# Two graph layers on one core: other places for ScalarE's copies, three last additions, the value products and the third pair's score tiles

## The chip, the cores and the metric

One core of one Trainium2 chip runs the whole kernel. The time is the device time of one execution in microseconds (us). Engines: TensorE (PE in the profile, its weight loads PEld), VectorE (DVE), ScalarE (ACT), GpSimd (POOL) and SyncE (SP, which issues the DMAs).

## The reference

There are 16 graphs of 512 nodes with 384 features, and two layers that are each added to their input. In outline:

```python
h = relu(layernorm(x));  x = x + attention(h, adj)
h = relu(layernorm(x));  x = x + graph_attention(h, adj)

# attention: 6 heads of 64 features
scores = q @ k.T / 8;  probs = softmax(where(adj, scores, -9e15))
out = (probs @ v) @ Wf + bf

# graph_attention: 12 heads of 32 features
hh = h @ W;  src = tanh(hh) . w_src;  dst = tanh(hh) . w_dst
attn = softmax(where(adj, leaky_relu(src_i + dst_j, 0.2), -999))
feat = elu(attn @ hh + b);  gate = sigmoid(h @ H_w.T + H_b)
out = gate * feat + (1 - gate) * h
```

## The kernel before, in words

The loop over graphs is software-pipelined. For graph b, `layer2(b)` runs the second layer, and in its spare places the first layer's query products, value products and first score tiles of graph b + 1. Then `attention(b + 1)` runs the first layer's attention, and in its spare places the end of graph b (the elu and the gate) and the key products of graph b + 2. There is one such round per graph. Each engine has its own program, written out by hand in the same function names, and waits on semaphores: an engine does its steps strictly in the written order.

The names that matter here, with the engine that does each step:

- The six heads of the attention are three **pairs** p = 0, 1, 2, and the 512 nodes four **tiles** t. `scores(g, p, t)` (PE, L1156) makes the two score tiles of a pair, called s(p,t) below; `maxima` (DVE, L822, two instructions) adds the mask and takes the row maximum; `exps` (ACT, L576, two instructions) takes the exponential and its sum; `inverse` (DVE, L828) inverts the sum; `normalise` (POOL, L416, two instructions) multiplies by it.
- `turn_probs(p, c)` (PE, L1173, 16 small transposes), called turn(p,c) below, turns column block c of the pair's probabilities into two PSUM banks, work0 and work1. DVE and ACT each empty one of them with a `pT_copy` (L832 and L582), and `context(p, c)` (PE, L1190, four matmuls), called ctx(p,c), multiplies by the values. The next turn needs both copies, since there is one pair of banks. `ctx_high` (ACT, L588) and `ctx_low` (DVE, L838) split a pair's result in two.
- `turn_norm` (PE, L1114), `turned_high` (ACT, L550) and `turned_low` (DVE, L799) turn the normalised input of the next graph; `query_key(p, "k")` (PE, L1099, nine matmuls) makes its keys, k0 to k2, which `qk_hi_copy` (ACT, L557) and `qk_low` (DVE, L807) split.
- The end of a graph, per tile: `positive` (DVE, L886), `elu` (ACT, L601), `difference` (DVE, L891), `add_out` (POOL, L458 and L460, the last addition) and a store.
- In `layer2`: `gate_product` (PE, L1099), `spread` (PE, L1233), 12 aggregation steps n, each with `edges` (DVE, L867, three instructions), `last_maxima` (ACT, L614 and L617), `last_edge` (POOL, L450) and `aggregate` (PE, L1252 and L1258, 16 matmuls); after the steps `sums_copy` (ACT, L625), `turn_sums(t)` (PE, L1271), `inverse_den` and `divide` (DVE, L873 and L878). `values(t)` (PE, L1099, nine matmuls of 384 columns) makes the next graph's values, and `value` (ACT, L562) empties them. `tanh_gate` is L605.

Eight PSUM banks hold everything. `HOME` (L41) says which of six shared banks a result goes to, and the lists `LAYER2` (L88) and `S_AFTER` (L62) in which order a bank's users follow each other; each user waits until the user before it has been drained. Values 3 and the sums of tile 1 share bank 0, values 2 and the sums of tiles 2 and 3 share bank 1.

In PE's program the scores of the next pair are spread over the turns by a table, and only the first turn of a pair waits for the probabilities, for all eight of them at once:

```python
S_AFTER = {(0, 0): ((1, 1), (1, 2)), (0, 1): ((1, 3),), (0, 3): ((2, 0), (2, 1)), (1, 0): ((2, 2),), (1, 1): ((2, 3),)}
...
                if c == 0:
                    pe.wait_ge(probs_ready, b * NS + tile_no(p, TT - 1, 1) + 1)
```

## Time and profile before

| | |
|---|---|
| median of 3 runs | 1788.58 us (1787.78 to 1788.93) |
| profiled execution, its own time | 1789.52 us |
| its span in the profile | 1787.7 us |
| busy: PE, DVE | 1669.8 us (93%), 1331.6 us (74%) |
| busy: ACT, POOL | 1102.6 us (62%), 1035.6 us (58%) |
| mean granted TensorE clock | 0.991 of full speed |

The profile is of one execution, and times in it count from the span's start. The busy time of an engine is the sum of its instructions; matmuls overlap, so PE's busy share is no measure of how much of its peak is used. What a step costs is read in the timeline: when it began, how long the engine had been idle before it, and for whom it had waited.

### The profile page before, as it was taken

How to read it: one execution, taken by the hardware profiler on the slowest of the kernel's cores; microseconds unless marked ns; L12 is line 12 of the kernel's file. 1: busy time of each engine (PE TensorE's matmuls, PEld its weight loads, DVE VectorE, ACT ScalarE, POOL GpSimd, SP SyncE). 2: the span in 40 equal slices, each digit the busy share in tenths (PEclk: the TensorE clock that was granted, in tenths of full speed). 3: DMA queues.
4: the chain of work that ended last, by engine and by line, in shares of the span. 5: the costliest groups of instructions: out<-in, count | busy, mean ns of one | idle time of the engine just before them, and what ended most of it. 6: DMA issues, size and time to landing. Idle time of an engine off the chain costs nothing.

```text
span 1787.7 us, 34621 instructions
## 1 busy us (share of the span) xinstructions
PE 1669.8 (93%) x12528; PEld 1021.7 (57%) x12528; DVE 1331.6 (74%) x3130; ACT 1102.6 (62%) x2231; POOL 1035.6 (58%) x1287
## 2 busy tenths in 40 slices
PE   6899999999999999999999999999999999999885
PEld 4474655647465574655657465574655746556462
DVE  4778687786878768677786877768777786876856
ACT  2666566675666656566665666666566665666653
POOL 4356565674656656565564646646575565655735
PEclk9899999999999999999999999999999999999997
DMA  4000101001010010100001010010100101000000
GB/s 156 19 19 11 50 7 37 19 16 45 7 54 7 15 40 8 54 7 25 30 12 50 7 37 25 11 44 7 54 7 15 41 12 50 7 19 19 10 10 18
DMA packets 38248, 48.24 MB, mean 27 GB/s; under 512 B 2624, under 2 KB 38080, under 8 KB 38080
## 3 DMA queue, kind: packets, MB, share of 16 engines
q1 hardware_dynamic: 38080, 46.03, 8.0%
q8 instruction: 102, 1.67, 0.4%
q14 instruction: 66, 0.54, 0.1%
HBM read 33.44 MB, written 12.58 MB: 26 GB/s over the span
## 4 chain that ended last, share of the span: by engine, by line
PE 74%; DVE 12%; ACT 6%; issue 3%; POOL 2%; DMA 0%; SPq 0%; DVEq 0%; POOLq 0%
PE work L1099 16%; PE score L1099 16%; PE acc L1258 8%; PE acc L1190 6%; PE acc L1252 6%; PE score L1156 6%; ACT arena L576 5%; PE work L1173 5%; DVE arena L867 4%; DVE sm L822 3%; PE work L1252 3%; POOL arena L416 2%; PE acc L1211 2%; PE score L1233 2%; PE score L1114 1%
## 5 line engine op out<-in xcount | busy, mean ns | idle before, releaser
L867 DVE SCALAR_TENSOR_TENSOR arena<-score,uqT,adjT 128x512 f32<-128x512 f32 x576 | 389.2, 745 | 33.3 <-PE score L1233 22.7
L416 POOL TENSOR_SCALAR arena<-arena,rinv 128x512 f32<-128x512 f32 x384 | 280.3, 746 | 186.1 <-DVE rinv L828 186.1
L576 ACT ACTIVATE arena<-sm,nmax 128x512 f32<-128x512 f32 x384 | 273.3, 714 | 126.2 <-DVE nmax L822 124.9
L450 POOL TENSOR_TENSOR arena<-arena,adjT 128x512 f32<-128x512 f32 x192 | 223.9, 1166 | 122.6 <-ACT arena L617 118.3
L822 DVE CUSTOM_DVE_ANT_0 sm<-score,mask 128x512 f32<-128x512 f32 x384 | 247.6, 685 | 56.8 <-issue 30.2
L1173 PEld LDWEIGHTS work<-ident_f,arena 64*128 64x128 f32 x3072 | 114.8, 140 | 180.8 <-issue 180.8
L1258 PE MATMUL acc<-arena,u_den 128*3 128x512 f32 x1536 | 200.8, 592 | 0.0
L1190 PE MATMUL acc<-arena,v_tok 128*64 128x512 f32 x768 | 197.7, 614 | 0.0
L423 POOL TENSOR_TENSOR rstd<-var,mhalf 128x1 f32<-128x1 f32 x128 | 68.7, 549 | 218.2 <-DVE var L786 218.2
L614 ACT ACTIVATE arena<-score,nqT 128x512 f32<-128x512 f32 x192 | 129.9, 677 | 100.8 <-PE score L1233 73.3
L1173 PE MATMUL work<-ident_f,arena 64*128 64x64 f32 x3072 | 138.0, 229 | 55.3 <-ACT arena L582 34.2
L832 DVE COPY arena<-work 128x512 f32<-128x512 f32 x192 | 130.9, 682 | 63.8 <-PE work L1173 63.7
L582 ACT ACTIVATE arena<-work 128x512 f32<-128x512 f32 x192 | 112.7, 587 | 94.0 <-PE work L1173 92.5
L1252 PE MATMUL acc<-arena 128*32 128x512 f32 x1024 | 135.2, 599 | 11.4 <-DVE arena L867 9.5
L617 ACT ACTIVATE arena<-arena,uqT 128x512 f32<-128x512 f32 x192 | 138.8, 723 | 6.2
L458 POOL TENSOR_TENSOR fin_g<-arena 128x384 f32<-128x384 f32 x64 | 69.1, 1080 | 114.1 <-DVE arena L891 113.7
L1258 PEld LDWEIGHTS acc<-arena,u_den 128*3 128x3 f32 x1536 | 42.4, 86 | 117.8 <-issue 117.8
L443 POOL TENSOR_TENSOR arena<-arena,uqT 128x384 f32<-128x384 f32 x64 | 61.3, 957 | 80.8 <-DVE uqT L1016 80.8
L1156 PE MATMUL score<-qk_hi 64*128 64x512 f32 x384 | 95.0, 481 | 5.2 <-DVE nmax L822 3.8
L544 ACT ACTIVATE hn<-xres,shift,rstd 128x384 f32<-128x384 f32 x64 | 45.4, 710 | 78.4 <-DVE shift L791 77.0
L807 DVE SCALAR_TENSOR_TENSOR qk_lo<-score,bias_c,qk_hi 128x512 fp32r<-128x512 f32 x64 | 47.9, 749 | 51.5 <-ACT qk_hi L557 51.5
L799 DVE SCALAR_TENSOR_TENSOR hT_lo<-score,hT_hi 128x384 fp32r<-128x384 f32 x112 | 59.0, 552 | 30.3 <-ACT hT_hi L550 30.2
(168 smaller groups left out, 3954.5 us busy)
## 6 DMA issues: line engine op xcount, KB each, us to landing
x_in<-in_x SPq DMA_DIRECT2D x16, 768.0 KB, 4.8
xb<-in_x SPq DMA_DIRECT2D x16, 768.0 KB, 4.6
out_x<-xres SPq DMA_DIRECT2D x64, 192.0 KB, 1.9
adj_u<-in_adj SPq DMA_DIRECT2D x16, 256.0 KB, 2.8
arena<-in_wk SPq DMA_DIRECT2D x1, 576.0 KB, 6.2
arena<-in_wq SPq DMA_DIRECT2D x1, 576.0 KB, 7.2
arena<-in_wv SPq DMA_DIRECT2D x1, 576.0 KB, 8.6
arena<-in_wf SPq DMA_DIRECT2D x1, 576.0 KB, 9.6
```

The lines of the kernel that those rows point to most:

```text
L416: nc.gpsimd.tensor_scalar(pr, pr, rinv[:, p, t, i:i + 1], 1.0, ALU.mult, ALU.mult).then_inc(probs_ready, 1)
L450: nc.gpsimd.tensor_tensor(edge_at(n, HG - 1), t_ring[:, n % 2], adjT[:, n % TT], ALU.mult).then_inc(last_edge_ready, 1)
L576: nc.scalar.activation(probs[p % 2 * 2 + i][:, t], sm[:, n % NSM], ACT.Exp, scale=-1.0, bias=nmax[:, p, t, i:i + 1], accum_out=rsum[:, p, ...
L617: nc.scalar.activation(t_ring[:, n % 2], t_ring[:, n % 2], ACT.Identity, bias=uqT[:, c, DROW + h:DROW + h + 1]).then_inc(max_ready, 1)
L822: mark_drained(nc.vector.tensor_tensor_reduce(sm[:, n % NSM], bank_of(g, "s", p, t, i)[:], mask[:, t], 1.0, 3.0e38, ALU.add, ALU.min, nmax ...
L867: nc.vector.scalar_tensor_tensor(out=edge_at(n, j), in0=score[j][:], scalar=uqT[:, c, q:q + 1], in1=adjT[:, c], op0=ALU.max, op1=ALU.mult) ...
L1099: ins = nc.tensor.matmul(ps, l(c), r(c), start=(c == 0 and i == 0), stop=(c == FC - 1 and i == 2))
L1156: ins = nc.tensor.matmul(bank_of(g, "s", p, t, i)[:], l[rows, 0, p, q], r[rows, 1, p], start=(n == 0), stop=(n == len(terms) - 1))
L1173: ins = nc.tensor.transpose(bank_of(b, "turn", p, c, half)[:, at:at + DH0], probs[p % 2 * 2 + i][rows, t, c * P:(c + 1) * P], ident_f[rows ...
L1190: ins = nc.tensor.matmul(acc[p % 2][i * DH0:(i + 1) * DH0], v_tok[:, c, f:f + DH0], pT[c % 2][:, i], start=(c == 0), stop=(c == TT - 1))
L1252: ins = nc.tensor.matmul(num[j * DH1:(j + 1) * DH1], h_tok[:, c, f:f + DH1], edge_at(n, j), start=(c == 0), stop=(c == TT - 1), skip_group ...
L1258: ins = nc.tensor.matmul(acc[1][j * DH1:j * DH1 + NG], u_den[:, c, g, j], edge_at(n, j), start=(n == 0), stop=(n == STEPS - 1), skip_group ...
```

## The change

Nothing is computed in another way; steps change places, and one wait is cut in pieces.

- **Value products.** `values(0)` goes from after aggregation step 5 to before step 0, `values(1)` from after the loop to after step 5. ScalarE's `value(0)` and `value(1)` follow, and its three later `tanh_gate` steps go to after steps 2, 3 and 6. Values 0 get bank 0.
- **After the loop.** PE makes s(0,3) before the sums of tile 1, and the sums of tiles 1 and 2 one after the other before values 3; VectorE does the maxima of s(0,3) before the division of tile 1.
- **Score tiles.** The third pair's tiles s(2,0) to s(2,3) come one after each of turn(0,3), turn(1,0), turn(1,1) and turn(1,2); two used to follow turn(0,3).
- **Copies.** ScalarE alternates exps and `pT_copy`.
- **Last additions.** `positive`, `elu`, `difference` and `add_out` of tiles 1 to 3 move towards the third pair.
- **The first turn of a pair** waits for each probability tile before that tile's transposes, and turns no longer raise a counter after their waits.

```diff
...
 
+TANH_AT = {2: 1, 3: 2, 6: 3}
+
 SPREADS = (3, 0, 1, 2)
...
     ("k", 0): 2, ("k", 1): 3, ("k", 2): 5, ("q", 0): 1, ("q", 1): 4, ("q", 2): 1,
-    ("v", 0): 1, ("v", 1): 1, ("v", 2): 1, ("v", 3): 0,
+    ("v", 0): 0, ("v", 1): 1, ("v", 2): 1, ("v", 3): 0,
     ("out", 0): 3, ("out", 1): 4, ("out", 2): 5, ("out", 3): 0,
...
 
-S_AFTER = {(0, 0): ((1, 1), (1, 2)), (0, 1): ((1, 3),), (0, 3): ((2, 0), (2, 1)), (1, 0): ((2, 2),), (1, 1): ((2, 3),)}
+S_AFTER = {(0, 0): ((1, 1), (1, 2)), (0, 1): ((1, 3),), (0, 3): ((2, 0),), (1, 0): ((2, 1),), (1, 1): ((2, 2),), (1, 2): ((2, 3),)}
 NORM_AFTER = {(0, 2): (0, 1), (1, 2): (2, 3)}
...
              ("feat", 0), ("feat", 1), ("feat", 2), ("tok", 0), ("tok", 1), ("tok", 2), ("tok", 3),
-             ("gate", 0), ("gate", 1), ("uq", 0), ("gate", 2), ("gate", 3), ("q", 2), ("num", 1), ("v", 0)]
-          + both("s", 0, 0) + both("s", 0, 1) + [("v", 1), ("fin", 0)] + both("s", 0, 2) + [("v", 2), ("fin", 1)]
-          + both("s", 0, 3) + [("fin", 2), ("v", 3), ("fin", 3)] + both("s", 1, 0))
+             ("gate", 0), ("gate", 1), ("uq", 0), ("gate", 2), ("gate", 3), ("v", 0), ("q", 2), ("num", 1), ("v", 1)]
+          + both("s", 0, 0) + both("s", 0, 1) + [("fin", 0)] + both("s", 0, 2) + [("v", 2)] + both("s", 0, 3)
+          + [("fin", 1), ("fin", 2), ("v", 3), ("fin", 3)] + both("s", 1, 0))
 START_UP = ([("norm1", t) for t in range(TT)]
...
                     add_out(g - 1, 0)
-                normalise(g, 2, 0)
-                if fin:
-                    add_out(g - 1, 1)
-                for t in range(1, TT):
+                for t in range(TT):
                     normalise(g, 2, t)
                 if fin:
-                    add_out(g - 1, 2)
-                    add_out(g - 1, 3)
+                    for t in range(1, TT):
+                        add_out(g - 1, t)
 
...
                 exps(g, 1, 1)
-                exps(g, 1, 2)
                 pT_copy(g, 0, 1)
+                exps(g, 1, 2)
+                pT_copy(g, 0, 2)
                 exps(g, 1, 3)
...
                     elu(g - 1, 0)
-                pT_copy(g, 0, 2)
+                pT_copy(g, 0, 3)
                 if more:
...
                     turned_high(g + 1, 0, 1)
-                pT_copy(g, 0, 3)
                 exps(g, 2, 0)
-                if fin:
-                    elu(g - 1, 1)
-                exps(g, 2, 1)
 
                 pT_copy(g, 1, 0)
+                exps(g, 2, 1)
                 ctx_high(g, 0)
-                exps(g, 2, 2)
                 pT_copy(g, 1, 1)
-                exps(g, 2, 3)
-                if fin:
-                    elu(g - 1, 2)
+                exps(g, 2, 2)
                 pT_copy(g, 1, 2)
...
                     turned_high(g + 1, 0, 3)
+                exps(g, 2, 3)
                 pT_copy(g, 1, 3)
                 if fin:
-                    elu(g - 1, 3)
+                    elu(g - 1, 1)
+                    elu(g - 1, 2)
 
...
                     qk_hi_copy(g + 1, 0, "k")
+                if fin:
+                    elu(g - 1, 3)
                 pT_copy(g, 2, 1)
...
                     last_maxima(b, n)
-                    if n < 3:
-                        tanh_gate(b, n + 1)
+                    if more and n == 1:
+                        value(b + 1, 0)
+                    if n in TANH_AT:
+                        tanh_gate(b, TANH_AT[n])
                     if more and n == 4:
...
                     if more and n == 8:
-                        value(b + 1, 0)
+                        value(b + 1, 1)
                 if more:
...
                 if more:
-                    value(b + 1, 1)
                     exps(b + 1, 0, 1)
...
                 maxima(g, 1, 3)
+                pT_copy(g, 0, 2)
+                inverse(g, 1, 2)
                 if fin:
...
                     positive(g - 1, 0)
-                pT_copy(g, 0, 2)
-                inverse(g, 1, 2)
+                pT_copy(g, 0, 3)
+                inverse(g, 1, 3)
                 if fin:
                     difference(g - 1, 0)
-                inverse(g, 1, 3)
                 if more:
...
                     turned_low(g + 1, 0, 1)
-                pT_copy(g, 0, 3)
                 maxima(g, 2, 0)
-                if fin:
-                    positive(g - 1, 1)
-                maxima(g, 2, 1)
 
                 pT_copy(g, 1, 0)
+                maxima(g, 2, 1)
                 inverse(g, 2, 0)
-                if fin:
-                    difference(g - 1, 1)
-                maxima(g, 2, 2)
-                inverse(g, 2, 1)
                 pT_copy(g, 1, 1)
                 ctx_low(g, 0)
-                maxima(g, 2, 3)
-                inverse(g, 2, 2)
-                if fin:
-                    positive(g - 1, 2)
+                maxima(g, 2, 2)
+                inverse(g, 2, 1)
                 pT_copy(g, 1, 2)
-                inverse(g, 2, 3)
                 if fin:
-                    difference(g - 1, 2)
+                    positive(g - 1, 1)
+                maxima(g, 2, 3)
+                inverse(g, 2, 2)
                 if more:
                     turned_low(g + 1, 0, 2)
-                pT_copy(g, 1, 3)
-                if more:
                     turned_low(g + 1, 0, 3)
+                pT_copy(g, 1, 3)
+                inverse(g, 2, 3)
                 if fin:
-                    positive(g - 1, 3)
+                    positive(g - 1, 2)
+                    difference(g - 1, 1)
 
                 pT_copy(g, 2, 0)
+                if fin:
+                    difference(g - 1, 2)
+                    positive(g - 1, 3)
                 if more:
...
                 ctx_low(g, 1)
+                if fin:
+                    difference(g - 1, 3)
                 if more:
...
                 pT_copy(g, 2, 2)
-                if fin:
-                    difference(g - 1, 3)
                 pT_copy(g, 2, 3)
...
                 nc.vector.tensor_copy(denT, acc[1][:]).then_inc(den_drained, 1)
-                for t in range(TT):
-                    if more and t < TT - 1:
-                        maxima(b + 1, 0, t + 1)
-                    if more:
-                        inverse(b + 1, 0, t)
-                    inverse_den(b, t)
-                    divide(b, t)
+                if more:
+                    maxima(b + 1, 0, 1)
+                    inverse(b + 1, 0, 0)
+                inverse_den(b, 0)
+                divide(b, 0)
+                if more:
+                    maxima(b + 1, 0, 2)
+                    inverse(b + 1, 0, 1)
+                    maxima(b + 1, 0, 3)
+                    inverse(b + 1, 0, 2)
+                inverse_den(b, 1)
+                divide(b, 1)
+                inverse_den(b, 2)
+                divide(b, 2)
+                if more:
+                    inverse(b + 1, 0, 3)
+                inverse_den(b, 3)
+                divide(b, 3)
                 if more:
...
                     bank_free(pe, b, "turn", p, c, half)
-                if c == 0:
-                    pe.wait_ge(probs_ready, b * NS + tile_no(p, TT - 1, 1) + 1)
-                settle(pe)
                 for i in range(2):
                     for t in range(TT):
+                        if c == 0:
+                            pe.wait_ge(probs_ready, b * NS + tile_no(p, t, i) + 1)
                         for half in range(2):
...
                 gate_product(b, 3)
+                if more:
+                    values(b + 1, 0)
 
...
                     if more and n == 5:
-                        values(b + 1, 0)
+                        values(b + 1, 1)
                     if n in (1, 5):
...
                     scores(b + 1, 0, 1)
-                    values(b + 1, 1)
                 turn_sums(b, 0)
...
                     values(b + 1, 2)
-                turn_sums(b, 1)
-                if more:
                     scores(b + 1, 0, 3)
+                turn_sums(b, 1)
                 turn_sums(b, 2)
```

How the steps stand on two engines, at three places.

VectorE after the aggregation's steps, from the inverse for tile 1 on (`sm` takes the maxima, rden and work0 are the division's). Before:

```order
L828 RECIPROCAL rinv<-rsum 128x2
L873 RECIPROCAL rden<-work0 128x12
L878 TENSOR_TENSOR arena<-work0,rden 128x384
L822 ISA sm,nmax<-score2,mask 128x512
L822 ISA nmax 128x1
L822 ISA sm,nmax<-score3,mask 128x512
```

Now:

```order
L827 RECIPROCAL rinv<-rsum 128x2
L821 ISA sm,nmax<-score2,mask 128x512
L821 ISA nmax 128x1
L821 ISA sm,nmax<-score3,mask 128x512
L821 ISA nmax 128x1
L827 RECIPROCAL rinv<-rsum 128x2
L872 RECIPROCAL rden<-work0 128x12
L877 TENSOR_TENSOR arena<-work0,rden 128x384
```

The division of tile 1, which frees bank 0 (work0), now stands behind both maxima of s(0,3) and the inverse for tile 2.

ScalarE in the second pair, from the exps of s(2,2) on (L576 and L575 are exps, L582 and L581 the copies, the rows into hT1_hi the turned input, those from arena to arena of 128x384 the elu). Before:

```order
L576 ACTIVATE arena,rsum<-sm,nmax 128x512 x2
L582 ACTIVATE arena<-work1 128x8x64
L576 ACTIVATE arena,rsum<-sm,nmax 128x512 x2
L601 ACTIVATE arena<-arena 128x384
L582 ACTIVATE arena<-work1 128x8x64
L550 ACTIVATE hT1_hi<-score2 128x3x128
L550 ACTIVATE hT1_hi<-score3 128x3x128
L582 ACTIVATE arena<-work1 128x8x64
```

Now:

```order
L575 ACTIVATE arena,rsum<-sm,nmax 128x512 x2
L581 ACTIVATE arena<-work1 128x8x64
L549 ACTIVATE hT1_hi<-score2 128x3x128
L549 ACTIVATE hT1_hi<-score3 128x3x128
L575 ACTIVATE arena,rsum<-sm,nmax 128x512 x2
L581 ACTIVATE arena<-work1 128x8x64
L600 ACTIVATE arena<-arena 128x384 x2
```

The first of these exps now comes one copy later, behind that of turn(1,1), and the last exps stand behind the copy of turn(1,2) and the turned input, directly ahead of the copy of turn(1,3).

VectorE in the third pair, from the copy of turn(2,0) on (L832 and L831 are the copies, qk_lo from score the keys' low halves, from acc1 the second pair's `ctx_low`, L891 and L890 the difference, L885 the positive part). Before:

```order
L832 COPY arena<-work0 128x8x64
L807 SCALAR_TENSOR_TENSOR qk_lo<-score0,bias_c,qk_hi 128x512
L832 COPY arena<-work0 128x8x64
L838 SCALAR_TENSOR_TENSOR qk_lo<-acc1,bias_c,qk_hi 128x512
L807 SCALAR_TENSOR_TENSOR qk_lo<-score1,bias_c,qk_hi 128x512
L832 COPY arena<-work0 128x8x64
L891 SCALAR_TENSOR_TENSOR arena<-arena 128x384
L832 COPY arena<-work0 128x8x64
```

Now:

```order
L831 COPY arena<-work0 128x8x64
L890 SCALAR_TENSOR_TENSOR arena<-arena 128x384
L885 SCALAR_TENSOR_TENSOR arena<-arena,hn 128x384
L806 SCALAR_TENSOR_TENSOR qk_lo<-score0,bias_c,qk_hi 128x512
L831 COPY arena<-work0 128x8x64
L837 SCALAR_TENSOR_TENSOR qk_lo<-acc1,bias_c,qk_hi 128x512
L890 SCALAR_TENSOR_TENSOR arena<-arena 128x384
L806 SCALAR_TENSOR_TENSOR qk_lo<-score1,bias_c,qk_hi 128x512
L831 COPY arena<-work0 128x8x64 x2
```

A difference now stands between `ctx_low` and the low half of k1, ahead of the copy of turn(2,2), where it stood behind that copy.

## Rows read from the trace of the kernel before

**Rows 1.** Busy time by stage, sum of one round (646 to 754 us).

```profile
sum 108.00, PE 103.65 PEld 63.45 DVE 82.42 ACT 68.35 POOL 64.46; mean PE 14.81 PEld 9.06 DVE 11.77 ACT 9.76 POOL 9.21
```

**Rows 2.** Timeline of PE, last gate product to aggregation: start, duration, [idle before <-releaser].

```profile
662.82 0.34 PE L1099 MATMUL work<-hw_hi,hT_lo 128*128 128x384 f32 x1
663.75 1.07 PE L1252 MATMUL acc<-arena 128*32 128x512 f32 x8 [0.59 <-DVE arena L867]
664.61 1.07 PE L1258 MATMUL acc<-arena,u_den 128*3 128x512 f32 x8
665.80 1.07 PE L1252 MATMUL acc<-arena 128*32 128x512 f32 x8
...
667.65 0.50 PE L1099 MATMUL work<-hT_hi,wq_hi 128*128 128x512 f32 x1
```

**Rows 3.** Timeline of PE, after the aggregation's steps to the first turn.

```profile
692.24 0.50 PE L1156 MATMUL score<-qk_hi 64*128 64x512 f32 x2
...
693.13 0.44 PE L1099 MATMUL work<-wv_hi,hT_hi 128*128 128x384 f32 x1
...
694.83 0.49 PE L1271 MATMUL work<-ident_f,arena 128*128 128x128 f32 x3
...
701.84 0.55 PE L1271 MATMUL work<-ident_f,arena 128*128 128x128 f32 x3 [0.21 <-DVE arena L878]
...
702.42 0.51 PE L1156 MATMUL score<-qk_hi 64*128 64x512 f32 x2
...
704.21 0.71 PE L1173 MATMUL work<-ident_f,arena 64*128 64x64 f32 x16 [0.81 <-POOL arena L416]
```

**Rows 4.** Timelines of DVE, ACT and POOL in the same stretch.

```profile
693.42 0.69 DVE L822 CUSTOM_DVE_ANT_0 sm<-score,mask 128x512 f32<-128x512 f32 x1 [0.35 <-PE score L1156]
...
694.03 0.69 DVE L822 CUSTOM_DVE_ANT_0 sm<-score,mask 128x512 f32<-128x512 f32 x1
...
701.22 0.56 DVE L878 TENSOR_TENSOR arena<-work,rden 128x384 f32<-128x384 f32 x1
...
691.36 0.72 ACT L576 ACTIVATE arena<-sm,nmax 128x512 f32<-128x512 f32 x1 [3.79 <-DVE nmax L822]
...
692.79 0.58 ACT L625 ACTIVATE arena<-acc 128x512 f32<-128x512 f32 x1
...
701.26 2.69 POOL L416 TENSOR_SCALAR arena<-arena,rinv 128x512 f32<-128x512 f32 x4 [1.77 <-DVE rinv L828]
```

**Rows 5.** Timeline of PE in the attention: turn(0,2), k0, turn(2,3).

```profile
710.09 0.71 PE L1173 MATMUL work<-ident_f,arena 64*128 64x64 f32 x16 [0.81 <-ACT arena L582]
...
726.94 0.50 PE L1099 MATMUL score<-hT_hi,wk_hi 128*128 128x512 f32 x1
...
735.68 0.71 PE L1173 MATMUL work<-ident_f,arena 64*128 64x64 f32 x16
```

**Rows 6.** Timeline of ACT in the attention: copies, turned input, exps of s(2,0).

```profile
709.42 0.57 ACT L582 ACTIVATE arena<-work 128x512 f32<-128x512 f32 x1
...
712.20 0.85 ACT L550 ACTIVATE hT_hi<-score 128x384 fp32r<-128x384 f32 x2
...
714.97 0.72 ACT L576 ACTIVATE arena<-sm,nmax 128x512 f32<-128x512 f32 x1 [1.04 <-DVE nmax L822]
...
718.91 0.68 ACT L588 ACTIVATE qk_hi<-acc,bias_c 128x512 fp32r<-128x512 f32 x1
...
725.16 0.60 ACT L582 ACTIVATE arena<-work 128x512 f32<-128x512 f32 x1
```

**Rows 7.** Timeline of DVE in the attention: two differences, the copy of turn(2,2); POOL's normalise.

```profile
718.18 0.53 DVE L891 SCALAR_TENSOR_TENSOR arena<-arena 128x384 f32<-128x384 f32 x1
...
723.87 0.84 DVE L891 SCALAR_TENSOR_TENSOR arena<-arena 128x384 f32<-128x384 f32 x1
...
734.85 0.68 DVE L832 COPY arena<-work 128x512 f32<-128x512 f32 x1
...
721.98 4.62 POOL L416 TENSOR_SCALAR arena<-arena,rinv 128x512 f32<-128x512 f32 x6
```

26 lines of the change are left out of this document (13 added, 13 removed).

## The prediction

> **What bounds the kernel now.** I read the busy time by stage first, then PE's timeline through one round, then the engine that PE waits for at each gap. A round (one graph) takes 108.00 us and PE is busy for 103.65 of them [rows 1], so PE sets the pace and a change can win at most its gaps, some 4.3 us. The reader is to see where these gaps lie. One is 0.59 before the first aggregation step [rows 2]. One is 0.81 before the first turn, where PE waits for POOL's last normalise [rows 3]. One is 0.81 before turn(0,2), where PE waits for ScalarE's copy, which stands behind two pairs of exps [rows 5]. The others, before turns of the second pair, are of the same kind. In the attention PE therefore hands work to DVE and ACT and waits to have it back: there the time of a step is the time of the chain through all three, and I replay that chain with durations from the rows. All times below are on the clock of the round shown.
>
> **Prices.** A value product: 694.83 - 693.13 = 1.70. A half aggregation step: 664.61 - 663.75 = 0.86, so 1.72 whole, and 667.65 - 665.80 = 1.85 with the switch to the next product [rows 2, 3]. A score tile to the next PE step: 0.89; to the begin of its maxima: 1.18; the second maximum starts 0.61 later, so a pair costs 1.22. One tile's sums to the next PE step: 702.42 - 701.84 = 0.58. A divide to the PE step that needs its bank: 701.84 - 701.22 = 0.62. A pair of exps to the next ACT step: 692.79 - 691.36 = 1.43. A normalise pair: half of 2.69, 1.35 [rows 3, 4]. ScalarE's copy to the turn that needs it: 710.09 - 709.42 = 0.67; DVE's: 735.68 - 734.85 = 0.83. A turn takes 0.71, and its copies start some 0.05 later [rows 5 to 7].
>
> **Value products (before step 0 and after step 5).** PE is free at about 662.82 + 0.18 = 663.00 and had to wait until 663.75. With values 0 there, step 0 starts at 663.0 + 1.70 = 664.70. Step 1, which had waited too (665.80, where 663.75 + 1.72 = 665.47 was possible), follows without a wait at 666.42, and the query product starts at 668.28 instead of 667.65: **+0.63** up to the end of the loop. The product's price is hidden for 1.07 of its 1.70. ScalarE now waits for values 0 ahead of its third step; that step's result is needed 6 us later, so I cost it at nothing, and the moved tanh steps too (they fill ScalarE's waits for spreads; their price, if that cover were gone, is one half step of ScalarE).
>
> **After the loop.** The scores of tile 1 start at 692.24 + 0.63 = 692.87. The sums of tile 0 had been covered by values 1; now they wait for ScalarE's sums copy, 692.79 + 0.63 = 693.42, plus 0.67 = 694.09. Then s(0,2) at 694.67, values 2 at 695.56, s(0,3) at 697.26, the sums of tiles 1 and 2 at 698.15 and 698.73, done at 699.3. Here PE needs bank 0, which the division of tile 1 must drain, and that stands behind the maxima of s(0,3): these begin at 697.26 + 1.18 = 698.44 and end at 699.66; with two small inverses (0.35 together, an estimate from the 0.2 to 0.3 steps around them) the divide starts at 700.0, and values 3 at 700.62: **a new PE stall of 1.3**. Sums of tile 3 at 702.32, s(1,0) at 702.90, first turn at 703.79. Before, these were 702.42 and 704.21 [rows 3]. POOL's last normalise no longer holds the turn: the divide of tile 2 ends at 701.3, an inverse and a hand-over later (some 0.4) POOL has its last pair, 1.35, so to 703.0. One value product less after the loop gives 1.70, less 0.63, less the two stalls of 0.3 and 1.3, plus the 0.81 that PE no longer waits for POOL: the turn gains 0.42, the scores s(1,0) lose 0.48.
>
> **First pair.** The next steps hang on the maxima of s(1,0), 702.90 + 1.18 = 704.08. On DVE follow two maxima to 705.3, the copy to 706.0, four maxima to 708.44, an inverse and the copy of turn(0,1) from 708.52: turn(0,2) can start at 709.35. ScalarE's copy, no longer behind a second pair of exps, is there earlier (exps of s(1,1) from 706.7 to 708.15, then copy, + 0.67 = 708.8), and PE, with a score tile and a context after turn(0,1), arrives at 709.35 as well. Against 710.09 [rows 5]: **-0.74**. This carries to turn(0,3).
>
> **Second pair.** The gain is spent. Now turned_high stands behind the copy of turn(0,3), turned_low behind turned_high, and the maxima of s(2,0) behind turned_low: turn(0,3) 711.8, copies at 712.55, turned_high 713.05 for 0.85, turned_low to 714.65, exps of s(2,0) at 715.4 against 714.97 [rows 6], though its scores are made earlier. Each later tile is made one turn later and alternates with a copy: copy of turn(1,0) at 716.85, exps of s(2,1) at 717.45, ctx_high at 718.9 (before: 718.91). DVE waits for it with ctx_low (an estimate of 0.7, from ctx_high's 0.68), and only then come the maxima of s(2,2), at 720.3, and its exps at 721.0, where ScalarE has waited a microsecond. Then copy (0.57, overlapped by 0.1), turned_high (0.85), exps of s(2,3) (1.43), and the copy of turn(1,3) at 725.2. Before: 725.16 [rows 6]. The last context of the pair needs that copy, and k0 follows it: 726.9 against 726.94, **-0.05**. Both positives and elus that left this stretch were on engines that now wait, so they win nothing.
>
> **Third pair.** PE has two key products as cover, so copies are late only at the end. The difference of tile 3 now stands before k1's low half and so before the copy of turn(2,2). DVE is without a pause from turn(2,1)'s copy to there (copy, ctx_low, low half, copy; before, PE had waited 0.2 for the last). So its 0.53 [rows 7], overlapped by some 0.08, comes on top: turn(2,3) goes from 735.68 to 736.1, **+0.45**. From here to the aggregation PE is dense. POOL's normalise of the third pair no longer stands behind an addition; it ends near 727.4, and turn(2,0) comes at 729.2, so it hides. The addition of tile 1 and its store come some 7 us later, the last ones no later, since the difference of tile 3 comes earlier; on SP's queue the next x stands behind them, which DVE reads half a round later. So I cost these at nothing; if that cover were gone, VectorE's next residual would wait for the last store.
>
> **The sum.** -0.05 + 0.45 = +0.40 a round, in 15 rounds (the last has no next graph): +6.0. The profiled execution took 1789.52 (span 1787.7 and 1.8 around it), so it would be 1795.5; the median of the runs, 1788.58, lies 0.94 lower, so I forecast **1794.6**. Over a chain of some forty links I allow 0.3 a round either way: 1790 to 1799 for this case alone. A measurement of this kernel tells 0.2% (3.6 us, 0.24 a round) from no change.
>
> **Two prices the trace doesn't show.** First, a turn whose transposes wait one by one. Eight satisfied waits cost between nothing and the time of a pair of transposes each, 2 x 0.71/16 = 0.09 [rows 5]; I take nothing, since the waits stand between pairs that PE issues while others run. Second, DVE beside POOL: a difference takes 0.53 at 718.18 and 0.84 at 723.87, in the middle of six normalise instructions [rows 7]. The difference of tile 0 now stands in the chain ahead of the maxima of s(2,0), at 713.2, and whether a normalise runs just then I can't tell; I take 0.53, and 0.31 more as the other end.
>
> The Trainium skill, page "SBUF — State Buffer", section "Who interferes with whom", says that VectorE and GpSimd share a port pair under an exclusive lock, so that the one that comes second waits out the other's whole instruction. By that rule a difference that meets a normalise would be late by up to 0.67 us, and the sum would be 15 x 0.67 = 10 us higher, 1804.7; the rows show a third of a microsecond, so the trace bears out that they meet, not the full size.
>
> **The rivals.** (a) *Faster*: the second pair doesn't spend the gain. For it: ScalarE has two elus less there. Against it: the waits for ctx_low and turned_low. It decides at the exps of s(2,2): begun by 720.3 instead of 721.0, k0 keeps the first pair's 0.74, and a round gains 0.74 - 0.45 = 0.3: 1784 (1780 to 1787). (b) *No change*: as forecast up to k0, but PE comes to turn(2,3) late enough that the difference is covered; then 1788 to 1789. Against it: DVE has no pause there. (c) *Slower by the shared port*: 0.31 more a round in front of the maxima of s(2,0), +0.7 in all: 1799. (d) *Slower by the small waits*: turns (1,0) and (2,0) are on the path; 8 x 0.09 x 2 = 1.4 a round at most: up to 1816.
>
> **How the numbers follow.** Forecast 0.47, (a) 0.20, (b) 0.18, (c) 0.10, (d) 0.05. Slower by over 0.2% holds (c), (d) and 0.40 of the forecast's 0.47 (its low end is within 0.2%): 0.55. Same: (b), the rest of the forecast and the edge of (a): 0.26. Faster: 0.19. The range goes from the middle of (a), 1782, through (c) to a part of (d), 1803.
>
> **What would show it.** Right: PE idle of over 1 us before values 3, waiting for a divide; turn(0,2) with hardly a wait; a PE wait of about 1 us before turn(1,1) and before the last context of the second pair; 0.6 before turn(2,3). A round of 108.4. Wrong: values 3 without a wait, or k0 more than 0.4 off its place, or the 16 transposes of a pair's first turn well above 0.71.

## The result and the profile after

The change is slower, as forecast and a little less so: a median of 1792.68 us (15 runs, 1790.97 to 1794.16) beside 1788.64 us of the kernel before on the same chip (15 runs, 1787.53 to 1790.31), a ratio of 1.0022, interval 1.0014 to 1.0029. The forecast was 1794.6.

I measure a round from one transposition of `uq_rows` on PE, between the gate products of tiles 1 and 2, to the next; the profile has 16 of these marks. The first of the 15 rounds between them is the same (108.31 before, 108.33 after). The 13 that follow last 107.96 to 108.03 us before and 108.22 to 108.30 after, one of them 108.60: **+0.25 a round**, where 0.40 was forecast. The last, whose attention has no next graph behind it, goes from 105.38 to 106.20. The first mark is 0.99 earlier (117.09 for 118.08), but two later runs with the same program up to there have it at 118.08 and 118.15, and a third, which differs only in its waits, at 118.07, so I count that as spread of the start and not as a term. In all, 4.5 - 1.0 = 3.5, which is the difference of the two spans (1791.2 and 1787.7 us).

Two terms that the working doesn't have lie in this start and cancel. The first score tile begins at 39.84 instead of 41.89: with values 0 in bank 0, PE waits only once, 0.58 us, before the start-up's value products, where it had waited 1.65 and twice 0.58. But from there to the first mark, over the first attention, the change takes 77.25 us (78.06 and 78.09 in the two later runs) and the kernel before 76.19.

Busy time of one round of the change, the same stretches as in [rows 1]; PE is busy 0.4 us less in the same 108 us:

```profile
sum 108.00, PE 103.25 PEld 62.87 DVE 81.05 ACT 68.09 POOL 63.98; mean PE 14.75 PEld 8.98 DVE 11.58 ACT 9.73 POOL 9.14
```

Timeline of PE after (start, duration, what it is, idle before it and what ended that), the same round as in [rows 2, 3, 5]; this round begins at 658.46, before at 658.35, so 0.11 is to be taken off each start:

```profile
664.78 1.06 PE L1258 MATMUL acc<-arena 128*32 128x512 f32 x8
...
694.13 0.55 PE L1277 MATMUL work<-ident_f,arena 128*128 128x128 f32 x3 [0.21 <-ACT arena L624]
...
700.73 0.45 PE L1106 MATMUL work<-wv_hi,hT_hi 128*128 128x384 f32 x1 [1.36 <-DVE arena L877]
...
702.95 0.51 PE L1163 MATMUL score<-qk_hi 64*128 64x512 f32 x2
...
703.99 0.68 PE L1179 MATMUL work<-ident_f,arena 64*128 64x64 f32 x15
...
709.42 0.71 PE L1179 MATMUL work<-ident_f,arena 64*128 64x64 f32 x16
...
715.14 0.71 PE L1179 MATMUL work<-ident_f,arena 64*128 64x64 f32 x16
...
717.56 0.71 PE L1179 MATMUL work<-ident_f,arena 64*128 64x64 f32 x16 [0.96 <-ACT arena L581]
...
725.89 1.08 PE L1196 MATMUL acc<-arena,v_tok 128*64 128x512 f32 x4 [0.69 <-DVE arena L831]
726.90 0.50 PE L1106 MATMUL score<-hT_hi,wk_hi 128*128 128x512 f32 x1
...
736.02 0.71 PE L1179 MATMUL work<-ident_f,arena 64*128 64x64 f32 x16 [0.50 <-DVE arena L831]
```

The L1179 rows are turn(0,0), turn(0,2), turn(1,0), turn(1,1) and turn(2,3). The first aggregation step no longer waits, as its 0.59 of idle time is now a value product. The new wait is there: 1.36 us before values 3, ended by a divide. turn(0,0) is 0.33 earlier in its round than before and s(1,0) 0.42 later; turn(0,2) has no wait and is 0.78 earlier; turn(1,1) waits 0.96 for ScalarE's copy, ctx(1,3) 0.69 for VectorE's; k0 is 0.15 earlier, and turn(2,3), with a wait of 0.50 that it did not have, 0.23 later.

Timelines of DVE and ACT after, the rows that end these waits (compare [rows 4, 6, 7]):

```profile
698.57 0.69 DVE L821 CUSTOM_DVE_ANT_0 sm<-score,mask 128x512 f32<-128x512 f32 x1 [1.03 <-PE score L1163]
...
700.12 0.56 DVE L877 TENSOR_TENSOR arena<-work,rden 128x384 f32<-128x384 f32 x1
...
713.31 0.54 DVE L890 SCALAR_TENSOR_TENSOR arena<-arena 128x384 f32<-128x384 f32 x1
...
725.16 0.68 DVE L831 COPY arena<-work 128x512 f32<-128x512 f32 x1
...
734.15 0.55 DVE L890 SCALAR_TENSOR_TENSOR arena<-arena 128x384 f32<-128x384 f32 x1
```

```profile
715.42 0.72 ACT L575 ACTIVATE arena<-sm,nmax 128x512 f32<-128x512 f32 x1 [1.40 <-DVE nmax L821]
...
721.07 0.72 ACT L575 ACTIVATE arena<-sm,nmax 128x512 f32<-128x512 f32 x1 [0.94 <-DVE nmax L821]
...
725.13 0.59 ACT L581 ACTIVATE arena<-work 128x512 f32<-128x512 f32 x1
```

The divide of tile 1 (700.12) stands behind the maxima of s(0,3), which VectorE had waited 1.03 for. The difference of tile 3 (734.15) stands in front of the copy of turn(2,2). The difference of tile 0 took 0.54: no collision. With the 0.11 taken off, the exps of s(2,2) begin at 720.96 and ScalarE's copy of turn(1,3) at 725.02; the working had 721.0 and 725.2. VectorE's copy of turn(1,3), behind the two `turned_low`, begins 0.03 later than ScalarE's and takes 0.68 for 0.59, and it is the one that ctx(1,3) waits for.

### The profile page after: what moved, and what is told of

Read it like the earlier page. It is cut to its first block, busy times and chain, and to the rows that moved or that the text cites. A ratio compares the mean times of both kernels' runs of the same rounds, so it can differ in the third digit from the quotient of the medians.

```text
span 1791.2 us, 34573 instructions
## 1 busy us (share of the span) xinstructions
PE 1667.4 (93%) x12528; PEld 1016.4 (57%) x12528; DVE 1315.1 (73%) x3130; ACT 1102.8 (62%) x2231; POOL 1033.5 (58%) x1287
## 4 chain that ended last, share of the span: by engine, by line
PE 74%; DVE 12%; ACT 6%; issue 6%; POOL 1%; DMA 0%; DVEq 0%; SPq 0%; POOLq 0%
PE work L1106 19%; PE score L1106 16%; PE acc L1264 7%; PE acc L1196 6%; PE acc L1258 5%; PE score L1163 4%; PE work L1179 4%; ACT arena L575 4%; DVE sm L821 3%; PE work L1258 3%; PE score L1239 2%; DVE arena L866 2%; DVE arena L831 2%; PE acc L1217 2%; PE score L1121 2%
## 5 line engine op out<-in xcount | busy, mean ns | idle before, releaser
L575 ACT ACTIVATE arena<-sm,nmax 128x512 f32<-128x512 f32 x384 | 273.5, 714 | 140.5 <-DVE nmax L821 138.7
L1179 PEld LDWEIGHTS work<-ident_f,arena 64*128 64x128 f32 x3072 | 113.8, 139 | 168.0 <-DVE arena L831 89.3
L831 DVE COPY arena<-work 128x512 f32<-128x512 f32 x192 | 131.4, 684 | 82.2 <-PE work L1179 81.1
L1179 PE MATMUL work<-ident_f,arena 64*128 64x64 f32 x3072 | 138.9, 229 | 43.2 <-ACT arena L581 27.6
L581 ACT ACTIVATE arena<-work 128x512 f32<-128x512 f32 x192 | 112.8, 587 | 96.3 <-PE work L1179 95.4
L1106 PE MATMUL work<-wv_hi,hT_hi 128*128 128x384 f32 x192 | 70.0, 364 | 21.2 <-DVE arena L877 20.7
L1196 PEld LDWEIGHTS acc<-arena,v_tok 128*64 128x64 f32 x768 | 40.0, 135 | 72.2 <-DVE arena L831 39.1
```

Of the source, the lines that this page charges most:

```text
L575: nc.scalar.activation(probs[p % 2 * 2 + i][:, t], sm[:, n % NSM], ACT.Exp, scale=-1.0, bias=nmax[:, p, t, i:i + 1], accum_out=rsum[:, p, ...
L831: mark_drained(nc.vector.tensor_copy(pT_half[c % 2][:, :, 0], bank_of(b, "turn", p, c, 0).rearrange("p (a n) -> p a n", n=DH0)), b, "turn" ...
L1106: ins = nc.tensor.matmul(ps, l(c), r(c), start=(c == 0 and i == 0), stop=(c == FC - 1 and i == 2))
L1179: ins = nc.tensor.transpose(bank_of(b, "turn", p, c, half)[:, at:at + DH0], probs[p % 2 * 2 + i][rows, t, c * P:(c + 1) * P], ident_f[rows ...
L1196: ins = nc.tensor.matmul(acc[p % 2][i * DH0:(i + 1) * DH0], v_tok[:, c, f:f + DH0], pT[c % 2][:, i], start=(c == 0), stop=(c == TT - 1))
```

## The experiments

Each run stood beside runs of the kernel before on the same chip (medians 1788.85 to 1789.76). "Round" is the usual one of the 15 in the run's trace, "last" the last.

| kernel | round | last | median us | ratio to before, interval |
|---|---|---|---|---|
| before | 108.00 | 105.38 | 1788.6 | |
| the change | 108.25 | 106.20 | 1792.7 | 1.0022 [1.0014, 1.0029] |
| difference(3) back | 107.78 | 106.17 | 1786.7 | 0.9983 [0.9974, 0.9992] |
| layer 2 as before | 107.84 | 105.79 | 1789.1 | 0.9997 [0.9988, 1.0005] |
| one wait again | 108.43 | 108.28 | 1797.5 | 1.0047 [1.0034, 1.0059] |
| division ahead of maxima | 107.75 | 106.40 | 1785.0 | 0.9979 [0.9970, 0.9987] |
| difference(3) and layer 2 | 107.34 | 105.63 | 1781.7 | 0.9957 [0.9944, 0.9969] |
| the same, copy of turn(1,3) earlier | 106.53 | 107.39 | 1771.2 | 0.9900 [0.9886, 0.9913] |
| the change, three mends | 106.44 | 107.58 | 1767.2 | 0.9880 [0.9864, 0.9897] |
| before, first pair alone | 109.5, 108.5 | 105.44 | 1806.7 | 1.0096 [1.0082, 1.0110] |
| the same, difference(1) moved | 107.05 | 103.36 | 1774.2 | 0.9917 [0.9904, 0.9931] |
| the same, small waits | 106.66 | 103.36 | 1768.0 | 0.9883 [0.9868, 0.9897] |

### The difference of tile 3 put back

```diff
                 ctx_low(g, 1)
-                if fin:
-                    difference(g - 1, 3)
                 if more:
                     qk_low(g + 1, 1, "k")
                 pT_copy(g, 2, 2)
+                if fin:
+                    difference(g - 1, 3)
```

> The changed kernel with one step put back: the difference of tile 3 stands behind the copy of turn(2,2) again. Theory (the difference lies in VectorE's chain to that copy and costs its 0.47 us a round): turn(2,3) comes 0.4 earlier, its wait of 0.50 falls to 0.1, 15 rounds give -6 us, 1787. Rival (PE waits there for something else, or the time comes back in the next stage): 1792 to 1793.

Timeline of PE (this round begins at 657.07):

```profile
725.54 0.50 PE L1106 MATMUL score<-hT_hi,wk_hi 128*128 128x512 f32 x1
...
734.19 0.71 PE L1179 MATMUL work<-ident_f,arena 64*128 64x64 f32 x16
```

k0 stands at 68.47 of the round, as in the change (68.44), and turn(2,3) at 77.12 instead of 77.56, without the wait. The round is 0.47 shorter: all of the third pair's term, by one instruction moved.

### Layer 2 and the aggregation as before

```diff
-    ("v", 0): 0, ("v", 1): 1, ("v", 2): 1, ("v", 3): 0,
+    ("v", 0): 1, ("v", 1): 1, ("v", 2): 1, ("v", 3): 0,
...
                 gate_product(b, 3)
-                if more:
-                    values(b + 1, 0)
...
                     if more and n == 5:
-                        values(b + 1, 1)
+                        values(b + 1, 0)
...
                     scores(b + 1, 0, 1)
+                    values(b + 1, 1)
                 turn_sums(b, 0)
```

(with the orders of LAYER2, ScalarE's copies and VectorE's divisions that belong to it)

> The changed kernel with the second layer as before (value products, sums, divisions, tanh and bank of values 0), the attention as changed. Theory (the later scores s(1,0) carry through the first pair, the earlier first turn doesn't): 0.3 us a round less, 1788, with no PE wait of over 1 us before values 3. Rival (the earlier first turn, 0.33 a round, is what the part is worth): 1797.

Timeline of PE (this round begins at 659.75):

```profile
704.86 0.84 PE L1167 MATMUL work<-ident_f,arena 64*128 64x64 f32 x16
...
726.76 1.08 PE L1184 MATMUL acc<-arena,v_tok 128*64 128x512 f32 x4 [0.69 <-DVE arena L830]
```

turn(0,0) comes at 45.11, 0.42 before the change's 45.53, and ctx(1,3) at 67.01, 0.42 before its 67.43. What s(1,0) loses after the loop is handed through two pairs of turns without a loss or a gain. The round is 0.41 shorter. Of 15 x 0.41 = 6.1 us, 3.6 show in the time, since this run's first mark is 3.1 us later. Most of that comes from the banks: with those of before, PE waits in the start-up 1.66 and twice 0.58 us before value products, with the change's once 0.58, which makes 2.2 of the 2.7 us by which the first score tile starts later (42.57 for 39.84).

### One wait for all probabilities again

```diff
+                if c == 0:
+                    pe.wait_ge(probs_ready, b * NS + tile_no(p, TT - 1, 1) + 1)
+                settle(pe)
                 for i in range(2):
                     for t in range(TT):
-                        if c == 0:
-                            pe.wait_ge(probs_ready, b * NS + tile_no(p, t, i) + 1)
```

> The changed kernel with one wait for all eight probability tiles at a pair's first turn, as before. Theory (satisfied waits cost nothing; turn(1,0) would wait for POOL's last pair, 0.2 us a round): 1792 to 1796. Rival (the small waits are what the change lost): 1788 or less, and the 16 transposes of a first turn shorter than in the changed kernel.

The small waits are a gain. Without them a round is 0.18 longer, and the last round 2.08: there turn(2,0), with no key product ahead of it, waits 1.27 us for POOL's last normalise. That makes 1.28 up to the feature product, the one with Wf behind the attention (79.90 of the round for 78.62); the other 0.80 come behind it, where the granted clock is at 0.50 for 6.8 us in place of 3.4. The 1797.5 is over what I had expected at most, by that last round and by one of 110.29, in which the granted clock is at 0.50 for 3.4 us. In the change the 16 transposes of turn(1,0), each pair behind a wait of its own, take 0.71, like those behind one wait [rows 3]. This edit also lets each turn raise its counter again (`settle`); what part of the 0.18 that takes is not shown.

### The division of tile 1 ahead of the maxima of s(0,3)

```diff
                     inverse(b + 1, 0, 1)
-                    maxima(b + 1, 0, 3)
-                    inverse(b + 1, 0, 2)
                 inverse_den(b, 1)
                 divide(b, 1)
+                if more:
+                    maxima(b + 1, 0, 3)
+                    inverse(b + 1, 0, 2)
```

> The change with the inverse and division of tile 1 ahead of maxima(0,3) on VectorE instead of behind; all else as in the change. Theory (the wait of 1.36 us of PE before values 3 is the division standing behind the maxima, and it is what layer 2 costs): divide(1) can start at about 699.2 instead of 700.12, values 3 and s(1,0) come 0.9 us earlier, the exps of (0,3) 0.7 to 1.1 us later, which turn(0,0) has room for by waiting for tile 3 last; of this 0.4 us a graph reach the end (what layer 2 as before gives), and the time is 1784 to 1788. Rival: the normalisation of (0,3) becomes what turn(0,0) waits for, and the time is 1791 to 1797.

Timelines of PE and DVE (this round begins at 656.91):

```profile
698.32 0.44 PE L1107 MATMUL work<-wv_hi,hT_hi 128*128 128x384 f32 x1 [0.48 <-DVE arena L877]
...
701.97 0.82 PE L1180 MATMUL work<-ident_f,arena 64*128 64x64 f32 x16
```

```profile
697.71 0.56 DVE L877 TENSOR_TENSOR arena<-work,rden 128x384 f32<-128x384 f32 x1
```

The wait before values 3 is 0.48 instead of 1.36, the product comes at 41.41 of the round instead of 42.27, and turn(0,0) at 45.06 instead of 45.53. Of the later normalisation hardly anything is felt: the 16 transposes take 0.82 instead of 0.71, as only the last two wait for it. The round is 0.50 shorter, where all of layer 2 put back gave 0.41, so this one place is the whole price of the new layer 2.

### Both put back, and then the copy of turn(1,3) one step earlier

The first run has the two edits above together (layer 2 as before, difference(3) behind the copy).

> The change with both suspected losses taken out: layer 2 and the last steps of the aggregation as before (with the banks of before), and the difference of tile 3 behind the copy of turn(2,2) again. If the two terms are separate, as the first runs have them (0.41 and 0.47 us a graph), the rounds last 108.25 - 0.88 = 107.37 us, and the time is that of the run with layer 2 put back less 15 x 0.47: about 1782 us (1780 to 1784), faster than both kernels. The start is again some 3 us later than that of the change, since that comes with the banks. Rival: the two overlap (the time that either gives is spent in the same wait); then the rounds stay at 107.8 us and the time at 1787 to 1789.

The terms add up: 107.34 for the expected 107.37, and 1781.7 us for the expected 1782. The second has in addition:

```diff
-                exps(g, 2, 3)
                 pT_copy(g, 1, 3)
+                exps(g, 2, 3)
...
                 inverse(g, 2, 2)
+                pT_copy(g, 1, 3)
                 if more:
                     turned_low(g + 1, 0, 2)
                     turned_low(g + 1, 0, 3)
-                pT_copy(g, 1, 3)
                 inverse(g, 2, 3)
```

> The same, and in the second pair ScalarE and VectorE copy turn(1,3) one step earlier: ScalarE ahead of the exps of (2,3), VectorE ahead of the two turned_low. Theory (the order of copies among exps and lows sets when PE gets on, wherever it is): ctx(1,3) no longer waits 0.68 us for VectorE's copy, k0 and the whole third pair come about 0.7 us earlier, rounds of 106.7 us, the time about 1772 us (1769 to 1776). Rival: the exps of (2,3), 0.6 us later, make the normalisation of tile 3 the wait of turn(2,0); then k0 is early, turn(2,0) is not, the gain is under 0.2 us a graph and the time 1779 to 1784.

Timelines of PE and DVE (this round begins at 652.24):

```profile
717.48 1.96 PE L1184 MATMUL acc<-arena,v_tok 128*64 128x512 f32 x8
719.46 0.47 PE L1094 MATMUL score<-hT_hi,wk_hi 128*128 128x512 f32 x1
...
721.73 0.71 PE L1167 MATMUL work<-ident_f,arena 64*128 64x64 f32 x16
```

```profile
717.61 0.67 DVE L830 COPY arena<-work 128x512 f32<-128x512 f32 x1
...
723.09 1.28 DVE L889 SCALAR_TENSOR_TENSOR arena<-arena 128x384 f32<-128x384 f32 x1
```

The last contexts of the second pair run on from the turn without a wait, k0 stands at 67.22 of the round (68.03 in the run without this edit, 68.44 in the change), and turn(2,0), at 69.49, did not have to wait for the later exps. 0.81 a round. Both engines' copies moved, so the run doesn't tell them apart.

### The first pair's order alone, on the kernel before

```diff
                 exps(g, 1, 1)
-                exps(g, 1, 2)
                 pT_copy(g, 0, 1)
-                exps(g, 1, 3)
...
+                exps(g, 1, 2)
                 pT_copy(g, 0, 2)
...
+                exps(g, 1, 3)
...
                 exps(g, 2, 0)
-                if fin:
-                    elu(g - 1, 1)
                 exps(g, 2, 1)
 
                 pT_copy(g, 1, 0)
                 ctx_high(g, 0)
+                if fin:
+                    elu(g - 1, 1)
```

(and VectorE's copies, inverses, positives and difference(0) of that pair to suit)

This is not quite the change's order: here the turned input comes ahead of the last exps and of the copy of turn(0,3), in the change behind both. So the run shows what an order of this kind is worth with the old second pair, not the change's first pair by itself.

> The kernel before with the first pair's order alone changed: ScalarE's copies between exps, the turned input ahead of the last exps and of the copy of turn(0,3), the positive part and the difference of tile 0 behind the copies, the second pair's first two maxima next to each other; two score tiles still follow turn(0,3). Theory (in the change the gain of 0.74 at turn(0,2) is spent by the second pair's own order): here it is kept, 0.7 to 0.9 a round, 1775 to 1779. Rival (the second pair spends it in any order, because VectorE and ScalarE bound it): 1787 to 1789.

A miss, by 28 us and in the sign. The first pair did as expected (turn(0,2) 0.89 earlier); the loss is behind it. Timelines of DVE, ACT and PE in the second pair (this round begins at 663.73), and two windows of the busy time with PE's granted clock (the column before the last two):

```profile
722.10 0.69 DVE L832 COPY arena<-work 128x512 f32<-128x512 f32 x1
...
723.89 0.67 DVE L891 SCALAR_TENSOR_TENSOR arena<-arena 128x384 f32<-128x384 f32 x1 [1.02 <-ACT arena L601]
724.48 0.68 DVE L822 CUSTOM_DVE_ANT_0 sm<-score,mask 128x512 f32<-128x512 f32 x1
```

```profile
723.34 0.52 ACT L601 ACTIVATE arena<-arena 128x384 f32<-128x384 f32 x1
725.20 0.72 ACT L576 ACTIVATE arena<-sm,nmax 128x512 f32<-128x512 f32 x1 [1.35 <-DVE nmax L822]
...
726.63 0.57 ACT L582 ACTIVATE arena<-work 128x512 f32<-128x512 f32 x1
```

```profile
727.30 0.71 PE L1172 MATMUL work<-ident_f,arena 64*128 64x64 f32 x16 [1.87 <-ACT arena L582]
727.94 1.54 PE L1113 MATMUL score<-ident_f,x_in 128*128 128x128 f32 x6
729.41 1.98 PE L1189 MATMUL acc<-arena,v_tok 128*64 128x512 f32 x4
```

```profile
724.00:727.00 3.00, 1.43 (x8) 0.20 (x4) 3.00 (x8) 1.80 (x5) 2.92 (x5) 1.00 0.19 68
...
728.00:731.00 3.00, 3.00 (x11) 1.38 (x10) 2.84 (x8) 2.91 (x8) 3.00 (x4) 0.50 0.20 71
```

VectorE stands 1.02 before the difference of tile 1, which needs the elu of tile 1 on ScalarE, which I had moved behind a copy and `ctx_high`. Behind that difference wait the maxima of s(2,2), so ScalarE stands 1.35 before its exps, and PE 1.87 before turn(1,2). Then PE's granted clock goes to 0.50, the level of 1.2 GHz, from 728 to 731: six transposes take 1.54 (0.87 in the change) and four contexts 1.98 (1.08). That is 1.57 us more, of which 1.1 stay in the round. 10 of the 14 rounds before the last are of this kind (109.5 to 109.8). The other four last 108.5: PE waits the same 1.87 there, but the granted clock stays at 1.00.

To settle it, the difference moved:

```diff
-                if fin:
-                    difference(g - 1, 1)
                 maxima(g, 2, 2)
...
                 if fin:
+                    difference(g - 1, 1)
                     difference(g - 1, 2)
```

(and POOL's add_out of tile 1 from behind normalise(2,0) to behind normalise(2,3))

> The kernel before with the first pair's order of the change (the run that came out at 1806.7 instead of 1775 to 1779), and now the difference of tile 1 also moved behind maxima(2,3), next to that of tile 2, and GpSimd's additions of tile 1 behind the four normalisations. Theory for that miss: I had put elu(1) behind ScalarE's copy of turn(1,0) but left difference(1), which needs it, ahead of maxima(2,2): VectorE stood 1.02 us behind ScalarE, the exps of (2,2), the copy of turn(1,1) and turn(1,2) (wait 1.87 us) came late in a row, and the granted clock fell to 0.90 in the wait. Then now VectorE does not stand there, turn(1,2) comes about 1.4 us earlier, the granted clock is back at 0.98 or more for the whole run, and the time is 1774 to 1783. Rival: the loss lies in the first pair's order itself (two tiles of exps in one step, or the clock); then the time stays above 1798.

Timelines of PE and DVE (this round begins at 653.24):

```profile
715.38 0.71 PE L1169 MATMUL work<-ident_f,arena 64*128 64x64 f32 x16 [0.41 <-issue]
716.02 0.87 PE L1110 MATMUL score<-ident_f,x_in 128*128 128x128 f32 x6
...
720.89 0.50 PE L1095 MATMUL score<-hT_hi,wk_hi 128*128 128x512 f32 x1
```

```profile
712.31 0.67 DVE L820 CUSTOM_DVE_ANT_0 sm<-score,mask 128x512 f32<-128x512 f32 x1
```

The maxima of s(2,2) begin at 59.07 of the round (60.75 before the edit), turn(1,2) at 62.14 instead of 63.57, the six transposes are back at 0.87. The mean granted clock of the run is 0.991 (0.983 before the edit). k0 stands at 67.65 of its round, 0.94 earlier than in the kernel before. One difference in the wrong place, with the addition that follows from it, was worth 32 us here.

With the change's small waits on top:

> The kernel before with the first pair's order and the difference of tile 1 moved (1774.2 us), and now the small waits of the change in the first turns too. In that run turn(0,0) waits 0.81 us for GpSimd's last normalisation with everything behind it in the queue. Theory (the small waits cost nothing by themselves and give back part of that wait): 0.1 to 0.5 us a graph less, 1767 to 1773. Rival (the small waits are paid for on each of the 16 short products): no gain or up to 10 us slower, 1774 to 1784.

turn(0,0) no longer waits for POOL (0.81 in the run before) and comes at 45.10 instead of 45.86; of this 0.39 stay in the round.

### The change with its three losses mended

Division, difference(3) and the copies of turn(1,3), each by the diff shown above, all else as in the change.

> The change with its three losses mended each in its place and the change's banks and value products kept: divide(1) ahead of maxima(0,3), the difference of tile 3 behind the copy of turn(2,2), the copies of turn(1,3) one step earlier. If the terms add up, the rounds last 107.75 - 0.47 - 0.81 = 106.47 us, the last round some 1.7 us more than with the division alone (as the copy alone did to it), and the time is 1785.0 - 14 x 1.28 + 1.7 = about 1769 us (1766 to 1772). Since this keeps the banks of the change, its start should be about 1 to 2 us earlier than in the run with layer 2 as before. Rival: one of the three gives what another gave already; then the rounds stay above 106.8 us and the time is 1773 to 1780.

106.44 us a round for the expected 106.47: the three terms add up. This is the best of the kernels run, 1.2% under the kernel before. Its first mark is 3.9 us earlier than that of the run with layer 2 as before and the copy (115.38 and 119.28), where I had expected 1 to 2; its first score tile is 3.4 earlier (38.99 and 42.38). Of these 3.4, 2.2 are the banks: PE waits 1.66 and twice 0.58 before the start-up's value products there, and once 0.58 here. Some 1.0 more lie before the first of these products, where the two programs are the same, so that is spread of the start.

## Why the prediction was right

**Layer 2 and the stall before values 3.** Right in place and size: 1.3 forecast, 1.36 measured; turn(0,0) -0.42 forecast, -0.33 measured; s(1,0) +0.48 forecast, +0.42 measured. The run with the division moved shows the mechanism. The last sentence of that part of the working is wrong: its terms add up to 0.28 and not to 0.42, as it leaves out what PE had waited before the sums of tile 3 (0.21, [rows 3]) and some small steps. The starts that it replays do give 0.42.

**First pair.** turn(0,2) -0.74 forecast, -0.78 measured.

**Second pair.** The exps of s(2,2) at 721.0 and the copy at 725.2 came at 720.96 and 725.02, so rival (a) fell at the point that I had named for it. k0 came at -0.15 for -0.05. The working had followed ScalarE's copy to ctx(1,3) and left out VectorE's, which ended last; that the two begin together is luck. What the working did not say is how the -0.05 is made up, and the runs show that it is no fixed end of the pair. An order of the first pair much like the change's brings k0 forward by 0.94 with the old second pair, and by 1.27 with the small waits (67.32 for 68.59); 0.42 of the loss comes from s(1,0), handed through; and the copies of turn(1,3), behind exps and turned_low, cost 0.81. Together that is -0.04 for the -0.15 measured, and the rest stays open.

**Third pair.** +0.45 forecast for the difference of tile 3; put back alone, it moves turn(2,3) by 0.44 and the round by 0.47. Against the kernel before, the change lost 0.23 + 0.15 = 0.38 between k0 and turn(2,3). The waits show the mechanism: PE's, for VectorE's copy, is 0.50, and it was 0.12 before, where the working had read 0.2.

**The sum.** The terms mis-sized are k0 (0.10 too late in my working) and the third pair against before (0.07 too much), which leave 0.23 a round of the 0.40, where 0.25 was measured. The sum also takes 15 rounds for alike: 15 x 0.40 = 6.0 us were forecast; what came is 0.02 for the first, 13 x 0.25 = 3.25, 0.35 for the one longer round (its wait before values 3 is 1.71; what made it so was not tried) and 0.82 for the last, whose attention has no next graph. It is just there that the steps moved to the third pair have no cover. That the total comes so near the forecast is in part luck: the start's two terms, some 2 us less for the banks and 1 to 2 more for the first attention, are not in the sum and nearly cancel. Timelines of the last attention, turn(2,2) and the feature product on PE before, then PE, DVE, ACT and POOL after (the rounds begin at 1630.32 and 1633.04):

```profile
1702.31 0.72 PE L1173 MATMUL work<-ident_f,arena 64*128 64x64 f32 x16
...
1708.13 0.45 PE L1099 MATMUL score<-wf_hi,qk_hi 128*128 128x384 f32 x1 [1.56 <-DVE qk_lo L838]
```

```profile
1705.67 0.72 PE L1179 MATMUL work<-ident_f,arena 64*128 64x64 f32 x16 [1.12 <-ACT arena L581]
...
1711.66 0.44 PE L1106 MATMUL score<-wf_hi,qk_hi 128*128 128x384 f32 x1 [1.56 <-DVE qk_lo L837]
```

```profile
1703.12 1.36 DVE L885 SCALAR_TENSOR_TENSOR arena<-arena,hn 128x384 f32<-128x384 f32 x1
...
1705.66 1.18 DVE L890 SCALAR_TENSOR_TENSOR arena<-arena 128x384 f32<-128x384 f32 x1
1706.76 0.68 DVE L831 COPY arena<-work 128x512 f32<-128x512 f32 x1
```

```profile
1704.52 0.52 ACT L600 ACTIVATE arena<-arena 128x384 f32<-128x384 f32 x1 [1.26 <-DVE arena L885]
1704.95 0.58 ACT L581 ACTIVATE arena<-work 128x512 f32<-128x512 f32 x1
```

```profile
1702.72 1.34 POOL L462 TENSOR_TENSOR xres<-fin_g,xres 128x384 f32<-128x384 f32 x1
...
1705.42 1.00 POOL L462 TENSOR_TENSOR xres<-fin_g,xres 128x384 f32<-128x384 f32 x1
```

The feature product is 0.81 late in its round (78.62 for 77.81). Without key products POOL's additions run while VectorE does positive(3) and difference(3), which take 1.36 and 1.18 there, for 0.55 where they meet nothing; elu(3) waits 1.26 for the one, with ScalarE's copy of turn(2,1) behind it, and VectorE's copy of turn(2,2) stands behind the other. Up to turn(2,1) the change is 0.56 ahead there (69.78 for 70.34); at turn(2,2), which waits 1.12, it is 0.64 behind. So the mechanism of rival (c) does come, in a place that I had not looked at. I read this from the rows; no run moves these two steps alone. The earlier copy of turn(1,3), too, gains in each round and loses in the last (107.39 for 105.63): 0.74 up to the feature product, where turn(2,0) waits 1.46 for POOL's normalise, and 1.0 behind it, where the granted clock is at 0.50 for 6.8 us instead of 3.4.

**The rivals.** (b), the difference covered: no, PE waits 0.50 for VectorE there. (c), the port: no collision at the difference of tile 0 (0.54 at 713.31), but two in the last attention. In the usual round the change has fewer than the kernel before: two positive parts take 0.84 and 0.79 (at 711.02 and 722.23), where four positive parts (0.85, 0.90, 0.61, 0.75) and a difference (0.84) had met a normalise or an addition. (d), the small waits: they cost nothing, two runs, in both of which the turns' counter goes with them, show a gain of 0.18 and 0.39. A slip in the working: it calls 1782, the low end of its range, the middle of (a), but (a) goes from 1780 to 1787, with its middle at 1783.5; nothing hangs on it.

## What to carry to other kernels

Where engines hand work round in a ring, a delay of one link can arrive undiminished at the next engine that has cover (0.42 us here, over eight turns), so a change is costed by replaying the ring to that place, link by link, and an instruction that waits for another engine belongs behind what the ring needs, never in front of it. Moving a producer without its consumer on another engine's queue turned a gain of 0.95 us a round into a loss of 1.2 on average. A change that comes out even can be a sum of large terms of both signs: put its parts back one at a time, and keep those that pay.

## What the runs showed of the hardware that I had not expected

**A difference or positive part on VectorE that begins inside an instruction of POOL waits out the rest of it.** I had taken the 0.31 us by which a difference grew in [rows 7] for the size of a collision, below the full size. In the rows of the last attention above, POOL's addition of 1702.72 ends at 1704.06 and positive(3) at 1704.48; that of 1705.42 ends at 1706.42 and difference(3) at 1706.84: both times 0.42 later, whenever they began. So it is in the run with the earlier copy, where a difference (723.09, above) took 1.28 and ended at 724.37, 0.41 behind this addition:

```profile
722.94 1.02 POOL L462 TENSOR_TENSOR xres<-fin_g,xres 128x384 f32<-128x384 f32 x1
```

The 0.31 was such a rest too: of the six normalises of [rows 7], the one that runs as the difference of 723.87 begins ends at 724.30, and the difference at 724.71:

```profile
723.61 0.69 POOL L416 TENSOR_SCALAR arena<-arena,rinv 128x512 f32<-128x512 f32 x1
```

In the trace of the kernel before, all 79 differences and positive parts that begin inside an instruction of POOL end 0.40 to 0.42 behind it. As such a step takes 0.53 to 0.55 alone, a collision costs what is left of POOL's instruction less some 0.13: 0.6 to 0.8 us in the three cases above, 0.3 in [rows 7]. Where VectorE began first, POOL waits: a normalise that begins at 713.59, inside the difference of tile 0, takes 0.81 for 0.69. Whom VectorE's next step finds ahead of it then differs: the normalise that begins at 726.11, inside a positive part, takes 1.20, and the difference of 726.29 goes ahead of it in 0.55, but positive(3) above waits behind an addition that had itself begun inside a difference (1702.66). What decides that is not shown. The Trainium skill, page "SBUF — State Buffer", section "Who interferes with whom", says of the two engines' shared ports that "it's an exclusive lock". These rows agree with it to within that 0.13, where my prediction had held the rows against it.

**A single wait of PE can cost more than itself, and not each time.** After 1.87 us without work the granted clock was 0.50, the level of 1.2 GHz, for some 3 us (rows of the first pair's run), which cost 1.57 us, in 10 of 14 rounds; in the other four the same wait left it at 1.00, as the wait of 1.36 before values 3 does in the change. The last round shows it too: from the feature product on, the kernel before and the change take 27.57 us and have 3.4 us at 0.50; five of the later runs have the same three waits there (some 0.75, 0.76 and 2.44), but 6.8 us at 0.50, and take 28.13 to 28.70.
